# A convolution and clustering block on one core: the second pass of the clustering spread over the next quarter's units, turning and aggregation in four column tiles, and the MLP tensors stored as overlapping 32-row blocks

## The reference, cut to what matters

```python
# layer 0, the MLP (x2 is the output of the attention; mlp = 192 channels)
y = gelu(layernorm(x2) @ fc1_w + fc1_b)                  # 2 x 192 x 256 x 256
dw = gelu(conv5x5_depthwise(y) + dw_b)
x = x + (y + dw) @ fc2_w + fc2_b + x2                    # x1 in the kernel
# layer 1, for each image and each quarter (128 x 128 pixels), 4 heads of 24 channels
feat, value = conv1x1(groupnorm(x), f), conv1x1(groupnorm(x), v)
centers, value_centers = pool(feat), pool(value)         # 4 centres per quarter and head
sim = sigmoid(beta + alpha * l2norm(centers) . l2norm(feat))      # 4 x 16384 per head
sim = sim * (one-hot of the argmax over the 4 centres)
agg = (sim @ value + value_centers) / (sum(sim) + 1)
out = agg^T @ sim                                        # back to every pixel
x = x + conv1x1(out, proj)
```

## Time and profile before

| | |
|---|---|
| time, median of 3 runs | 8124.62 us (8104.56 to 8129.87) |
| the profiled execution's own time | 8155.58 us |
| its span in the profile | 8153.9 us |
| granted TensorE clock, mean | 0.942 |
| PE busy | 6772.1 us, 83% |
| DVE busy | 4893.0 us, 60% |
| HBM read and written | 731.05 and 432.51 MB |

### The profile page before, as it was taken

The page is one execution under the profiler, slowest core; times in us unless marked ns, Lnnn a source line. Parts: engine busy times, 40 slices in busy tenths (PEclk is TensorE's granted clock), DMA queues, the critical chain, the costliest instruction groups (busy, mean ns, idle before and its releaser), DMA issues. The chain is left out here.

```text
span 8153.9 us, 144011 instructions
## 1 busy us (share of the span) xinstructions
PE 6772.1 (83%) x52386; PEld 3497.3 (43%) x52386; DVE 4893.0 (60%) x7407; ACT 3594.3 (44%) x5633; POOL 2490.7 (31%) x3236
## 2 busy tenths in 40 slices
PE   0887999999999999999979978997577675776776
PEld 0333555555555555555433335554000003675665
DVE  6895777777777777777755557776122224334433
ACT  0554666666666666666546643333001013141231
POOL 0444444444444444444466610000122220000000
PEclk9997999999999999999999989998788887998999
DMA  7774433443333343333178878887999992334244
GB/s 297 205 227 94 90 79 74 89 90 73 84 84 74 78 89 86 73 85 84 29 192 230 244 208 271 276 275 246 222 256 239 257 245 70 119 93 143 83 129 135
DMA packets 487474, 1226.31 MB, mean 150 GB/s; under 512 B 163749, under 2 KB 168741, under 8 KB 461989
## 3 DMA queue, kind: packets, MB, share of 16 engines
q1 hardware_dynamic: 444180, 1116.09, 52.8%
q10 hardware_dynamic: 28368, 51.91, 2.0%
q0 software_dynamic: 14336, 50.34, 1.7%
HBM read 731.05 MB, written 432.51 MB: 143 GB/s over the span
## 5 line engine op out<-in xcount | busy, mean ns | idle before, releaser
L727 DVE TENSOR_REDUCE at_mz<-at_ps 128x4 bf16<-128x1024 f32 x1444 | 1774.3, 1229 | 781.8 <-PE at_ps L651 781.5
L600 ACT ACTIVATE at_E<-at_ps 128x1024 f32<-128x1024 f32 x1444 | 1500.7, 1040 | 793.8 <-PE at_ps L663 793.8
L663 PE MATMUL at_ps<-at_qaug,at_k 32*128 32x256 f32 x11552 | 830.2, 401 | 78.2 <-DVE at_qaug L751 78.2
L1181 PE MATMUL cv_ps<-cv_yin,cv_band 128*128 128x384 f32 x2304 | 787.1, 503 | 116.4 <-DMA cv_yin<-y_mlp 116.4
L1201 DVE TENSOR_TENSOR cv_yin<-cv_gl,cv_yin 64x384 f32<-64x384 f32 x1152 | 637.4, 553 | 282.3 <-ACT cv_gl L1192 274.5
L674 PE MATMUL at_ps<-at_E,at_vaug 128*32 128x256 f32 x11552 | 774.3, 386 | 0.0
L1287 POOL TENSOR_TENSOR f_xa<-f_xa,f_xb 128x3840 f32<-128x3840 f32 (+1 forms) x28 | 212.8, 7620 | 1761.1 <-DMA f_xb<-in_x 1761.1
L663 PEld LDWEIGHTS at_ps<-at_qaug,at_k 32*128 32x128 f32 x11552 | 523.2, 184 | 442.2 <-issue 224.5
L1307 PE MATMUL f_ps<-f_sa,f_wa 128*32 128x512 f32 (+1 forms) x1728 | 380.3, 959 | 353.8 <-DMA f_sbb<-s_mlp 353.8
L1181 PEld LDWEIGHTS cv_ps<-cv_yin,cv_band 128*128 128x128 f32 x2304 | 449.2, 196 | 454.6 <-DMA cv_yin<-y_mlp 139.4
L1326 DVE SCALAR_TENSOR_TENSOR f_xa<-f_ps,f_b,f_xa 128x512 f32<-128x512 f32 (+1 forms) x216 | 136.1, 686 | 840.1 <-PE f_ps L1310 840.1
(11 more groups left out here) (207 smaller groups left out, 10123.5 us busy)
## 6 DMA issues: line engine op xcount, KB each, us to landing
cl_xu<-x SPq DMA_DIRECT2D x256, 384.0 KB, 3.4
cv_yin<-y_mlp SPq DMA_DIRECT2D x96, 1023.8 KB
s_mlp<-cv_yin SPq DMA_DIRECT2D x96, 950.6 KB
at_rows_in<-y_attention SPq DMA_DIRECT2D x38, 1536.0 KB, 9.4
gn_xin<-in_x SPq DMA_DIRECT2D x16, 3072.0 KB, 22.9
ln_xin<-in_x SPq DMA_DIRECT2D x192, 256.0 KB, 7.4
y_attention<-ln_xin SPq DMA_DIRECT2D x192, 256.0 KB, 3.8
out<-cl_ou POOLq DMA_DIRECT2D x128, 384.0 KB, 3.9
```

Of the source, the lines that this page charges most:

```text
L600: act.activation(E[:, m % 2, 2 * p:2 * p + 2, :], psum[:, 2 + 2 * p:4 + 2 * p, :], ACT.Exp).then_inc(exp_done, 1)
L663: i = pe.matmul(psum[:, 2 + h, TOK * j:TOK * j + TOK], k[rows, n % 2, tokens(w, 128 * j, 128)], qaug[rows, m % 2, :], start=True, stop=True)
L727: dve.tensor_reduce(mz[:, m % 2].rearrange("p j (h c) -> p h j c", c=32)[:, 2 * p:2 * p + 2, :, DQ], psum[:, 0:2, :].rearrange("p h (j n) ...
L1181: m = pe.matmul(psum[:, n % NB, 0:3 * RUN], band[:, s, c, a, :], yin[:, s, c, 3 * u:3 * u + 3, GAP * a:GAP * a + RUN], start=(a == 0), sto ...
```

## The change

The change has four parts.

1. **Layout of the MLP tensors.** `y_mlp` and `s_mlp` hold 32 rows for each of nine blocks (the last four of a block are the first four of the next one, held twice) in place of 28 rows of ten blocks. `fc1` stores rows 0 to 3 of a block a second time (`row_places`), `conv` loads a group in one transfer and stores it in one, and `fc2` reads rows 0 and 1 from the block before them (`row_sources`).
2. **Order of transfers** in `fc1` and `fc2`: `grp` outside, g in the order 0, 2, 1, 3.
3. **Clustering, column tiles.** A unit's eight tiles are turned by eight products of 16 columns, four at a time in the four column tiles of PE, and aggregated likewise into four partial sums. One more product with the matrix `combine` adds the two partial sums of each side. The second pass multiplies 16 rows by 512 pixels: two products, in two row tiles of PE, make a *piece* of 1024 pixels, where eight products of 128 pixels made them before.
4. **Clustering, order of work.** The loops are written out in full. The second pass of quarter f runs as 32 pieces: two behind the products of units 3 to 7 of segments 1 to 3 of quarter f + 1, and two in segment 0 of quarter f + 2. What has no place there, all 32 pieces of the last quarter and two of the one before, runs at the end. The turning of segment s - 1 goes behind the products of units 3 to 7 (`TURN_AT`). The input has three buffers for the first pass and three of its own, of twice the size, for the second; the result is written over the second one and stored 768 KB at a time.

The diff, cut to its core:

```diff
 def fc1(nc, p, x2, ydr):
-                for g in range(4):
-                    for grp in range(CGRP):
+                for grp in range(CGRP):
+                    for g in (0, 2, 1, 3):
...
                 for rr in range(2):
-                    row = r0 + 2 * rr + jj
-                    for f in range(2):
+                    for row, t, at, n in row_places(k, rr, jj):
+                        for f in range(2):
...
 def conv(nc, p, ydr, sdr, tdr, groups=MLP // 4):
-        LOADS = 1 + 2 * 2
-        STORES = 2 * 4
+        LOADS = 2
+        STORES = 1
...
-                for f in range(2):
-                    src = lines(ydr, g, f)
-                    lo = 64 * f
-                    sp.dma_start(tile(lo, lo + KEEP, s), src[:, :, 0:NBLK * PITCH]).then_inc(loaded[s], 16)
-                    sp.dma_start(tile(lo + KEEP, lo + 64, s), src[0:64 - KEEP, :, PITCH:]).then_inc(loaded[s], 16)
+                sp.dma_start(tile(s), lines(ydr, g)).then_inc(loaded[s], 16)
...
+                sp.dma_start(lines(sdr, g), tile(s)).then_inc(stored[s], 16)
...
 def cluster(nc, x1, out, t):
+    XS, XV, QS = 3, 3, 6
+    TURN_AT = (3, 3, 4, 4, 5, 5, 6, 7)
...
+            def load_pair(w):
+                if w >= XV:
+                    sp.wait_ge(stored[w % XV], 16 * (w // XV))
+                sp.dma_start(xv[:, w % XV, :], rows(x1, w // PAIRS, w % PAIRS * 2 * UROWS, 2 * UROWS)).then_inc(again[w % XV], 16)
...
+            for seg, u, turns, pieces in steps():
+                n = seg * UPS + u + XS - 1
+                if n < TOTAL:
+                    load(n)
+                pairs_after(pieces)
...
+            def turn(seg, w):
...
+                for i in range(2):
+                    for j in range(4):
+                        tile = NT * w + 2 * (2 * i + j % 2) + j // 2
+                        m = pe.matmul(turn_ps[32 * j:32 * j + EM, 128 * i:128 * i + 128], sm[:, seg % 2, tile, :], t["eye"][:], start=True, stop=True)
+                m.then_inc(tp_done, 1)
...
+                        m = pe.matmul(psum[32 * j:32 * j + EM, 4, 0:VC], sm[:, seg % 2, tile, :], val[:, seg % 2, tile, :],
+                                      start=False, stop=last and i == 1, skip_group_check=True)
...
+            def piece(f, i):
+                w, side = i // 2, i % 2
+                if i == 0:
+                    pe.wait_ge(lhs_out, f + 1)
+                if order(f, i):
+                    pe.wait_ge(y_out, order(f, i))
+                for a in range(2):
+                    j = 2 * side + a
+                    m = pe.matmul(psum[0:C, 6 + a, :], lhs[32 * j:32 * j + EM, f % 2, :], smt[32 * j:32 * j + EM, f % 2, 2 * w:2 * w + 2, :, :],
+                                  start=True, stop=True)
+                m.then_inc(y_done, 1)
+
+            for seg, u, turns, pieces in steps():
+                f, s = seg // SU, seg % SU
+                if seg < SEGS:
+                    products(seg * UPS + u)
+                for a in turns:
+                    turn(*a)
+                if f and s == 0 and u == UPS - 1:
+                    combined(f - 1)
...
+                if f and s == 1 and u == 0:
+                    turned(f - 1)
+                if f and s == 1 and u == 1:
+                    projected(f - 1)
+                for a in pieces:
+                    piece(*a)
+            for a in rest:
+                piece(*a)
...
         @block.vector
+            for seg, u, turns, pieces in steps():
+                f, s = seg // SU, seg % SU
+                if seg and u == 0:
+                    similar(seg - 1)
+                if seg < SEGS:
+                    norms(seg * UPS + u)
+                if seg and u == 0:
+                    choose(seg - 1)
+                for a in turns:
+                    turned(*a)
...
+                for a in pieces:
+                    added(*a)
```

More of the change, by code:

```diff
@@ L787 @@
 FIRST = BLK - 1 - TAPS // 2
-TBLK = NBLK + 1
 RUN = B * COLS
@@ L882, in fc1 @@
         LOADS = 4 * CGRP
-        STORES = 8
+        stores = [sum(4 * len(row_places(i, rr, 0)) for i in range(k) for rr in range(2)) for k in range(NTILE + 1)]
         def part(a, n, grp=slice(None)):
@@ L1233, in fc2 @@
         XLOADS = 4 * CGRP
-        SLOADS = 8
+        s_loads = [sum(4 * len(row_sources(i, rr, 0)) for i in range(k + 1) for rr in range(2)) for k in range(NTILE)]
         @block.sync
@@ L1607, in _, with steps, order @@
+        def steps():
+            for seg in range(SEGS + 1):
+                for u in range(UPS):
+                    turns = [(seg - 1, w) for w in range(UPS) if TURN_AT[w] == u] if seg else []
+                    yield seg, u, turns, pieces_at(seg, u)
+        rest = [(f, i) for f in range(HALVES) for i in range(2 * PAIRS)]
+        for _, _, _, some in steps():
+            rest = [r for r in rest if r not in some]
+        def order(f, i):
+            return f * 2 * PAIRS + i
         @block.sync
@@ new lines, in _, with pairs_after @@
+            for n in range(XS - 1):
+                load(n)
+            for w in range(XV - 1):
+                load_pair(w)
+            def pairs_after(pieces):
+                for f, i in pieces:
+                    w = f * PAIRS + i // 2 + XV - 1
+                    if i % 2 == 1 and w < HALVES * PAIRS:
+                        load_pair(w)
+            for seg, u, turns, pieces in steps():
+                n = seg * UPS + u + XS - 1
+                if n < TOTAL:
+                    load(n)
+                pairs_after(pieces)
@@ L1633, in _ @@
+            pairs_after(rest)
+        @block.gpsimd
+        def _(pool):
+            for w in range(HALVES * PAIRS):
+                pool.wait_ge(y_out, 2 * (w + 1))
+                pool.dma_start(rows(out, w // PAIRS, w % PAIRS * 2 * UROWS, 2 * UROWS), xv[:, w % XV, :]).then_inc(stored[w % XV], 16)
+            for i in range(XV):
+                pool.wait_ge(stored[i], 16 * len(range(i, HALVES * PAIRS, XV)))
         @block.tensor
@@ new lines, in _, with link, norms @@
+            linked = [0]
+            def link(ins):
+                linked[0] += 1
+                ins.then_inc(chain, 1)
+                dve.wait_ge(chain, linked[0])
+            def norms(n):
+                seg = n // UPS
+                for half in range(2):
+                    h = 2 * n + half
+                    dve.wait_ge(sq_done, h + 1)
+                    first = (n % UPS * NT + 4 * half) * CH_HEADS
+                    dve.tensor_reduce(n2[:, seg % 2, first:first + 4 * CH_HEADS], sqf[:, h % QS].rearrange("p t (e c) -> p (t e) c", c=CH_DIM),
+                                      AX.X, ALU.add).then_inc(n2_done, 1)
@@ new lines, in added @@
+            def added(f, i):
+                w, side = f * PAIRS + i // 2, i % 2
+                dve.wait_ge(y_done, order(f, i) + 1)
+                if side == 0:
+                    dve.wait_ge(again[w % XV], 16 * (w // XV + 1))
+                for a in range(2):
+                    x = xv[:, w % XV, :].rearrange("c (r a n) -> c r a n", a=4, n=128)[:, :, 2 * a + side, :]
+                    m = dve.scalar_tensor_tensor(out=x, in0=psum[0:C, 6 + a, :].rearrange("c (r n) -> c r n", n=128), scalar=t["proj_b"][:, 0:1], in1=x,
+                                                 op0=ALU.add, op1=ALU.add)
+                m.then_inc(y_out, 1)
```

463 lines of the change are left out of this document (228 added, 235 removed).

## The result

The changed kernel takes 7693.3 us, the median of 4 runs (7665.6 to 7714.0), against 8114.9 for the kernel before (8104.6 to 8129.9): a ratio of 0.947, 95% interval 0.944 to 0.949. The forecast was 7557. Its profiled execution took 7690.7 us, its span is 7688.9.

What follows compares the result with a forecast made beforehand. Transfers were taken to bind `fc2`, PE `fc1`, a chain of waits `cluster`; PE was busy most of `conv`. 8155.6 - 371 (`cluster`) - 147 (`conv`) - 55 (`fc2`) + 3 (`fc1`) = 7586, scaled to 7557 us; range 7440 to 7765.

Steps and rivals of the forecast that it cites:

- The scaling: Whole kernel: the sum of 7586 us times 8124.6 / 8155.6, since the profiled execution was 0.4% above the median, giving 7557.
- Clustering, the clock: In `cluster`: PE's time at the lower clock level, 1.2 GHz, would add between 0 and 54 us; 30 taken.
- The rival: In `cluster`: PE at 1.2 GHz in the 48 steps with pieces and at the end, 260 us more, 7815; chance 0.10.
- Clustering, the steps: In `cluster`: turning and aggregation 0.95 us, piece period 2.67; segments 55.5 us with pieces, 39.3 without, later segments 0 42.7.
- The term 34 x 2.67: End of `cluster`: 34 pieces, each waiting for the one before, 2.67 us apart, 91 us in all.
- The note that it would grow "by 21 us": End of `cluster`: if three buffers fail to cover the loads, the end grows to 34 x 3.3, by 21 us.
- A change of tiling: In `cluster`: by the skill's drain rule, 400 mode changes at an estimated 0.2 us would add 80 us; not taken.
- its lower bound: In `conv`: nothing waits, PE's 743 us plus head and tail make 781 us, 147 less; this was taken.
- the upper bound: In `conv`: today's rate of 269 GB/s carries 249 MB in 926 us, with head and tail 970 us.
- Order of the transfers: In `fc2`: the new order speeds up x2 and x loads, 0 to 80 us less, 55 taken.
- `fc1`: Stage `fc1`: second stores mostly hidden by two output buffers; 3 us more, bounds 5 less and 25 more.
- SP's queue: In `cluster`: loads behind stores on SP's queue delay 48 steps by 6 us each, 290 us; chance 0.03.

Runs made afterwards that it cites:

- the zeros: The kernel after with three products of zeros behind each step's first piece and behind each of the last 32 pieces; ratio to before 0.932, `cluster` 946 us.
- the cut transfers: The kernel after with each `conv` group's load cut into four transfers and its store into six, same bytes; one run, `conv` 928 us.
- the order alone: The kernel before with only the new order of transfers in `fc1` and `fc2`; ratio to before 0.991, `fc2` 1011 us.
- the one with pieces between the halves: The kernel after with each step's second piece put behind the first four products of the next unit; ratio to before 0.925, `cluster` 890 us.

## Why the prediction was off by 136 us, point by point

Between the profiled executions 570 us less were forecast and 465 came, 105 short. By stage: `cluster` and its setup lost 272 us and not 371, 99 short; `fc1` gained 17 and not 3, 14; the untouched stages ahead of it took 10 more (they end between 4074 and 4086 us in the fourteen profiles, and the kernel before has the 4074); `conv` was 13 us and `fc2` 5 us better than forecast. The forecast was then scaled down by 29 us to the median, and the profiled execution after lies 3 us below its own: together the 136. The 7693 lie inside the forecast's own range (7450 to 7700) by luck: `cluster` with 1055 us lies outside its 915 to 1050, and `conv` and `fc2` made up 18 us of it. The scaling itself was a step without ground: it took the 31 us by which the profiled execution before lay above its median for a share of everything, while `conv` with the old transfers differs by 39 us between executions and with the new ones took 767 to 769 us in all eight profiles. If the 31 us are those 39, which fits and is not shown, the sum of 7586 needed no scaling, and the gain of `conv` to be set against a median is some 120 us and not 147.

- **Clustering, the clock.** This step failed. It put the lower level at 30 us, from the mean clock of the stage before and "PE's gaps stay under 2 us". Both stand, PE's waits for a sum in a step are 1.5 us, and the clock fell all the same, to 0.72 to 0.82 in segments with pieces. Nine such segments took 619 us from one choice to the next (65 each for four of them, 70 to 73 for five, three of which also have the weights) where 514 were forecast, and the 34 pieces of the end came 3.53 us apart instead of 2.67, 29 us more: 134, of which the allowance covered 30. With the clock held up the stage took 946. The rival named this mechanism and gave it 0.10, with 260 us; it came at a little over half of that, since the products behind the waits ran slowly and most other work of a step did not.
- **Clustering, the steps.** Right: 0.89 us for a turning and aggregation, 2.61 for a piece, segments without pieces 39.8 us (39.3), segments of 54.9 with the zeros (55.5), where the clock is high, the segments 0 37.8 to 44.2 (42.7).
- **Clustering, the end.** The term 34 x 2.67 was mis-sized by 29 us. The note that it would grow "by 21 us" if the loads' cover fails was the nearer: with the clock up the loads of three buffers take over at nearly the same length.
- **A change of tiling.** The Trainium skill (TensorEngine Tiling (Array Packing), Key Properties) has it drain the engine. The traces here show no room for 0.2 us each: eight products, turning, aggregation and piece change tiling three times in a unit, and from a turning to its piece 0.89 us pass, of which the columns are 0.76; with the clock up a segment takes 54.9 us, less than the sum of 55.5, which had 0.2 us a turning for beginning and changing over together.
- **`conv`.** Right in the mechanism and in the length of the stage after: PE's 745 us, 768 in all against 781. The forecast took its lower bound, and the cut transfers show why it was the right one: the same bytes, cut much as before, bring the old wait back. The Trainium skill (DMA: Bandwidth & Descriptors, How many engines (k)) agrees with this: 56, 8, 52 and 4 partitions do not divide over 16 engines as 128 do. By that rule the forecast had the slowest engine carry 332 KB a group after the change; with the sizes of the rows it is 324. No row shows the single engines, and the number of transfers changed too, so the rule is a reading here and not shown. The 249 MB of the upper bound were some 3% low, as a KB of the rows is 1024 bytes (768 us at 333 GB/s are 256 MB); that bound was 993 and not 970.
- **Order of the transfers.** Right in the size: 56 us in `fc2` against 55, from the order alone. The forecast ascribed it to the loads; 17 us of it came from the stores of x1.
- **`fc1`.** Mis-sized, 17 us against 3, inside the bounds of 5 less and 25 more. The second stores are not hidden by two output buffers, because they stand behind a tile's loads: put ahead of them, they leave 5 of the 17 us.
- **SP's queue.** Right that it holds nothing back within the segments: no row has a piece waiting for its pair there.

## What to carry to other kernels

Work that is put into another loop's gaps is not placed well as long as an engine waits inside it: here each second piece waited 1.5 us for VectorE, and the larger part of the price was not the wait but the products after it at half the clock (with the waits kept and the clock back, 118 of the 171 us). Put a dependent pair apart, with independent work between (171 us here, from the place of one piece), and judge the place by the granted clock of the stretch, not by the length of the gaps. In `conv` one transfer of 128 partitions was worth more than several that add up to it, even though it moved more bytes; and in `fc2`, where transfers bind, their order on a queue was a cost of its own.

## What was not expected of the hardware

- TensorE's granted clock was 0.82 in stretches with PE busy for 53.6 of 65 us and no wait over 1.7 us, and 0.97 with three more products of zeros in each step, which finished the same work 10 us sooner. In two earlier segments with the same five waits of 1.5 us it was 0.74 and 0.72, and they took 71 and 72 us; no run here tells why.
- Within a step the time was lost in one place: a turning, an aggregation and a first piece took 0.63, 0.52 and 1.10 us in the kernel after and in the one with pieces between the halves; sixteen records of the products behind a waiting piece took 4.76 us in the first, and eight took 1.67 in the second.
- `conv` of the kernel before ran at 928 us in two profiles and at 889 and 891 in two others, with the same code for this stage and the same bytes; the waits for loads were 115 and 116 us in the first two and 93 and 97 in the others, and PE's busy time 786 to 787 against 768, so each makes up about half of the difference. No run here tells why.
